# Expert stages: where each engine reads the expert numbers it addresses its operands with

## The chip, the cores and the metric

The kernel runs on one core of a Trainium2 chip. The metric is the device time of one execution in microseconds (us); the time quoted for a kernel is the median of its runs. The engines are named as the profile names them: PE (matrix multiplication; PEld is its weight load), DVE (vector), ACT (activations and copies), POOL (here it issues indirect DMAs) and SP (here it issues DMAs). A name with a q behind it (DVEq, ACTq, SPq) is the part of an engine that reads its instruction stream: it hands work to the engine, and carries out register loads, register arithmetic and branches itself.

## The reference

A block of a network over x of shape 2 x 2048 x 128, in float32. The two `ffn` lines are mixtures of eight experts; each token takes two of them.

```python
x = x + attn_a(layernorm(x))     # windowed attention, 16 heads of 64
x = x + ffn(layernorm(x))        # experts, first time
x = x + attn_b(layernorm(x))     # full attention per batch
x = x + ffn(layernorm(x))        # experts, second time

def ffn(x, w_router, w1, b1, w2, b2):
    probs = softmax(x @ w_router)              # 8 experts
    topk_w, topk_idx = top_k(probs, 2)
    weights = sum(topk_w[..., None] * one_hot(topk_idx, 8), axis=1)
    h = gelu(einsum('te,ieh->tih', x, w1) + b1)   # 128 -> 512
    out = einsum('tih,ihe->tie', h, w2) + b2      # 512 -> 128
    return sum(out * weights[..., None], axis=1)
```

## The kernel before, in words

The stages follow one another: layer norm, windowed attention, an expert stage (`expert_stage`, tag 1), layer norm, full attention, a second expert stage (tag 3). A router inside the attention stages has by then sorted the tokens by expert into a DRAM buffer `xg`, in 40 groups of 256 rows (`GROUPS`), each group of one expert only, and has left two tables in on-chip memory: `emap[j]`, the expert of group j, and `gmap[j]`, the place of group j in `xg`. Which expert a group has is known only at run time, so an engine that addresses weights by it first reads the number from `emap` into a register of its own. `expert` (L1199) does that for DVE and ACT, `place` (L1202) reads `gmap` for SP. One such read is a TENSOR_LOAD, one or two register operations (FUSED_REGOPS) and a range test (SEQ_ASSERT); all of them stand in the trace under L1200 or L1203.

The 40 groups are cut into five turns of eight (`STEP`): turn 0 and turn 4 are written out, turns 1 to 3 are a hardware loop (`rounds`, L1189). `steps` (L1175) builds a turn for PE, ACT and DVE from a `body(jj, k)`. What the engines do for a group:

- SP fetches a group's rows into `xt`, five groups ahead, into one of eight buffers, once POOL's write of the buffer's former group has landed (L1211, L1219).
- PE transposes a group into `px` (L1256), multiplies it with the first weights into `ph` (L1265, 12 products per group) and the result with the second weights into `py` (L1283, 16 products). In body j it does `px` of group j+2, then `ph` of j+1, then `py` of j. There is one `px`, so the `px` of group j+2 waits until DVE has read group j+1's: `pe.wait_ge(S["xl"], START + j + 2)` (L1271).
- ACT copies `px` to `xh` (L1297) for group j+2 and then applies gelu with the expert's bias (L1302) for group j+1.
- DVE copies the expert's first weights to `w1s` (L1324, L1325) and forms `xl` from `px` and `xh` (L1329) for group j+2; then adds the second bias to `py` and scales the result, `yo` (L1337, L1342), for group j-1; then copies the second weights to `w2s` (L1333) for group j+1.
- POOL writes `yo` out with two indirect DMAs per group (L1242).

All this order is written out by hand; each engine runs its own instructions in that order, and semaphores are waited on as counts. Before the change, `turn` in `steps` reads every expert number that the turn needs in one row, before the first group's body: on DVE ten in turn 0, eleven in turns 1 to 3 and nine in turn 4; on ACT nine (eight in turn 4); on SP `turn` reads up to eight places first.

Of the kernel before, what the change touches and what calls it, by code (L numbers as in the profile page):

```python
# [28 lines left out]
STEP = 8  # L29
HCHUNKS = FFN // P  # L30
GROUP = 2 * P
GROUPS = TILES * P * TOPK // GROUP + EXPERTS
# [170 lines left out]
def fetch_outputs(sp, s, got):  # L203

    parts = s.yt.rearrange("(r t p) d -> r p t d", r=TOPK, p=P)
    for i in range(NSB):
        r = slice(i * SB_TILES, (i + 1) * SB_TILES)
        for k in range(TOPK):
            sp.dma_start(got[:, k, r, :], parts[k][:, r, :]).then_inc(s.fetched[i], 16)  # L209


def combine(nc, ch, s, got, i, nth):

    r = slice(i * SB_TILES, (i + 1) * SB_TILES)
    ch.eng.wait_ge(s.fetched[i], 16 * TOPK * nth)
    for k in range(TOPK):
        ch.link(nc.vector.tensor_tensor(s.x[:, r, :], s.x[:, r, :], got[:, k, r, :], ALU.add))  # L217
# [928 lines left out]
def expert_stage(nc, sems, tag, s, result=None):  # L1146
# [5 lines left out]
    with ExitStack() as ctx:  # L1152
        m = Memory(nc, ctx)
        LEAD = 5
# [17 lines left out]
        xg = s.xg[nth]  # L1172
        block = ctx.enter_context(nc.Block())

        def steps(eng, body, ahead=None, behind=False):  # L1175


            def turn(jj):
                es = []
                if ahead is not None:  # L1180
                    es = [expert(eng, STEP * jj + a) for a in range(STEP + ahead)
                          if not isinstance(jj, int) or STEP * jj + a < GROUPS]
                before = [expert(eng, STEP * jj - 1) if not isinstance(jj, int) or jj > 0 else None] if behind else []
                for k in range(STEP):
                    body(jj, k, *([es[k:]] if es else []), *([(before + es)[k]] if behind else []))

            rounds(eng, turn)

        def rounds(eng, turn):  # L1189
            turn(0)  # L1190
            with eng.Fori(0, ROUNDS - 2) as i:
                turn(i + 1)
            turn(ROUNDS - 1)

        def outside(jj, k, ahead):

            return isinstance(jj, int) and not 0 <= STEP * jj + k + ahead < GROUPS

        def expert(eng, j):  # L1199
            return eng.value_load(s.emap[0:1, bass.ds(j, 1)], min_val=0, max_val=EXPERTS - 1)  # L1200

        def place(eng, j):  # L1202
            return eng.value_load(s.gmap[0:1, bass.ds(j, 1)], min_val=0, max_val=XBLOCKS - 1)  # L1203

        def rows(dram, j):
            return dram[bass.ds(j, 1), :, :].rearrange("o (p r) d -> p (o r) d", r=GROUP // P)

        @block.sync
        def _(sp):
            def fetch(g, k):  # L1210
                sp.dma_start(xt[:, k, :, :], rows(xg, g)).then_inc(load[k], 16)  # L1211

            def turn(jj):
                gs = [place(sp, STEP * jj + LEAD + a) if not outside(jj, a, LEAD) else None for a in range(STEP)]
                for k in range(STEP):
                    if not outside(jj, k, LEAD):
                        if not outside(jj, k, LEAD - STEP):
                            was = k + LEAD - STEP
                            sp.wait_ge(put[was % STEP], 32 * (nth * ROUNDS + jj + 1 + was // STEP))  # L1219
                        fetch(gs[k], (k + LEAD) % STEP)  # L1220

            for k in range(LEAD):
                fetch(place(sp, k), k)
            rounds(sp, turn)
            if result is not None:
                for k in range(STEP):
                    sp.wait_ge(put[k], 32 * (nth + 1) * ROUNDS)
                fetch_outputs(sp, s, got)
                for i in range(NSB):
                    sp.wait_ge(summed, START + i + 1)  # L1230
                    r = slice(i * SB_TILES, (i + 1) * SB_TILES)
                    sp.dma_start(tokens[:, r, :], s.x[:, r, :]).then_inc(s.s_out, 16)
                sp.wait_ge(s.s_out, 16 * NSB)
# [59 lines left out]
        @block.scalar  # L1293
        def _(act):
            def read(j, k):
                act.wait_ge(S["t"], START + j + 1)
                nc.scalar.copy(xh[:, k % 2, :], px[:, 0:GROUP]).then_inc(S["xT"], 1)  # L1297

            def gelu(j, k, e):
                act.wait_ge(S["h"], START + j + 1)  # L1300
                for i in range(HCHUNKS):
                    nc.scalar.activation(hT[:, k % 2, i, :], ph[:, k % 2, i, :], ACT.Gelu_apprx_tanh,  # L1302
                                         bias=s.b1[:, bass.ds(e * HCHUNKS + i, 1)]).then_inc(S["gelu"], 1)

            def body(jj, k, es):
                j = STEP * jj + k
                if not outside(jj, k, 2):
                    act.wait_ge(S["h"], START + j + 1)
                    read(j + 2, k + 2)
                if not outside(jj, k, 1):  # L1310
                    if not outside(jj, k, -1):
                        act.wait_ge(S["y"], START + j)
                    gelu(j + 1, k + 1, es[1])

            e = expert(act, 0)
            read(0, 0)
            read(1, 1)
            gelu(0, 0, e)
            steps(act, body, 1)

        @block.vector
        def _(dve):
            def first_weights(j, k, e):
                nc.vector.tensor_copy(w1s[:, k % 2, 0, :], s.w1h[:, e, :])  # L1324
                nc.vector.tensor_copy(w1s[:, k % 2, 1, :], s.w1[:, e, :].bitcast(F32R)).then_inc(S["w1"], 1)  # L1325

            def low_x(j, k):
                dve.wait_ge(S["xT"], START + j + 1)
                nc.vector.tensor_tensor(xl[:, k % 2, :], px[:, 0:GROUP], xh[:, k % 2, :].bitcast(F32),  # L1329
                                        ALU.subtract).then_inc(S["xl"], 1)  # L1330

            def second_weights(j, k, e):
                nc.vector.tensor_copy(w2s[:, k % 2, :, :], s.w2[:, e, :, :]).then_inc(S["w2"], 1)  # L1333

            def keep(j, k, e):
                dve.wait_ge(S["y"], START + j + 1)
                nc.vector.tensor_tensor(yo[:, k % YBUF, :, :], py[:, k % 2, 0:GROUP].rearrange("p (r d) -> p r d", d=P),  # L1337
                                        s.b2[:, bass.ds(e, 1), :].to_broadcast([P, GROUP // P, HID]),
                                        ALU.add).then_inc(S["yb"], 1)
                dve.wait_ge(S["yb"], START + j + 1)  # L1340
                for r in range(GROUP // P):
                    ins = nc.vector.tensor_scalar(yo[:, k % YBUF, r, :], yo[:, k % YBUF, r, :],  # L1342
                                                  xt[:, k % STEP, r, HID + 1:], None, ALU.mult)
                ins.then_inc(S["yo"], 1)

            def body(jj, k, es, e_before):
                j = STEP * jj + k
                if not outside(jj, k, 2):
                    dve.wait_ge(S["h"], START + j + 1)
                    first_weights(j + 2, k + 2, es[2])  # L1350
                    low_x(j + 2, k + 2)
                if not outside(jj, k, -1):
                    if not outside(jj, k, -1 - YBUF):
                        was = k - 1 - YBUF
                        dve.wait_ge(put[was % STEP], 32 * (nth * ROUNDS + jj + 1 + was // STEP))
                    keep(j - 1, (k - 1) % STEP, e_before)
                if not outside(jj, k, 1):
                    if not outside(jj, k, -1):
                        dve.wait_ge(S["y"], START + j)
                    second_weights(j + 1, k + 1, es[1])  # L1360

            e0, e1 = expert(dve, 0), expert(dve, 1)
            first_weights(0, 0, e0)
            first_weights(1, 1, e1)
            low_x(0, 0)
            low_x(1, 1)
            second_weights(0, 0, e0)
            steps(dve, body, 2, behind=True)
            dve.wait_ge(put[(GROUPS - 1 - YBUF) % STEP], 32 * (nth * ROUNDS + (GROUPS - 1 - YBUF) // STEP + 1))
            keep(GROUPS - 1, GROUPS - 1, expert(dve, GROUPS - 1))  # L1370
            if result is not None:
                ch = Chain(dve, s.signals["last"]["chain"])
                for i in range(NSB):
                    combine(nc, ch, s, got, i, 2)
                    dve.sem_inc(summed, 1)
# [459 lines left out]
```

## Time and profile before

| | us |
|---|---|
| median of 3 runs | 1534.84 (1534.63 to 1535.37) |
| the profiled execution, its own time | 1529.88 |
| the profiled execution, its span | 1528.1 |
| busy: PE | 1273.1 (83%) |
| busy: DVE | 1043.8 (68%) |
| busy: ACT | 900.7 (59%) |
| busy: POOL | 763.8 (50%) |

The busy shares are means over stages with different limits. The two expert stages stand in the span from about 811 to 995 us and from about 1327 to 1500 us; what matters for the change is read there. The profile lists TensorE's granted clock as a share of its full 2.4 GHz; half of it is the lower level of 1.2 GHz.

### The profile page before, as it was taken

To read this page: it belongs to the slowest core of one execution; us is meant where nothing else is said; L and a number is where in the kernel's file an instruction comes from. 1 tells how busy PE (TensorE), PEld (TensorE's weight loads), DVE (VectorE), ACT (ScalarE), POOL (GpSimd) and SP (SyncE) were. 2 spreads that over 40 slices of the span, in tenths; PEclk is the share of its full clock that TensorE was granted. 3 is DMA by queue.
4 is the path that set the end of the run, shared out by engine and by line. 5 is a ranking of instruction groups with operands and counts; after the bars stand their busy time and mean duration, and the time that the engine had idled before them with its cause. 6 is when DMAs were issued, how large, how long until landed. Compare 5 with 4: busy or idle time off the path is not lost. (4 is left out here: it accounts for less than half of the span.)

```text
span 1528.1 us, 34022 instructions
## 1 busy us (share of the span) xinstructions
PE 1273.1 (83%) x9640; PEld 1004.4 (66%) x9640; DVE 1043.8 (68%) x3646; ACT 900.7 (59%) x2287; POOL 763.8 (50%) x798
## 2 busy tenths in 40 slices
PE   3999999999999999999956888629878885288892
PEld 2677766777666666766745888616765665288892
DVE  7666877878788787887854554476786788245564
ACT  2677767778686777777753444317655664144451
POOL 3676676686666857667633544400021422434452
PEclk9899999999999999999977999859989997598896
DMA  8999990000000000000031222030000000121226
GB/s 257 209 207 204 202 196 9 4 12 1 10 6 4 12 1 15 1 4 12 2 129 56 64 60 58 25 110 1 1 17 13 29 15 15 46 59 54 60 63 166
DMA packets 129396, 91.94 MB, mean 60 GB/s; under 512 B 9115, under 2 KB 122030, under 8 KB 128992
## 3 DMA queue, kind: packets, MB, share of 16 engines
q1 hardware_dynamic: 118080, 71.84, 21.7%
q0 software_dynamic: 9248, 16.94, 3.3%
q10 hardware_dynamic: 1920, 1.60, 0.3%
q8 instruction: 42, 0.69, 0.2%
q14 instruction: 106, 0.87, 0.2%
HBM read 30.86 MB, written 61.64 MB: 61 GB/s over the span
## 5 line engine op out<-in xcount | busy, mean ns | idle before, releaser
L923 DVE CUSTOM_DVE_ANT_0 sc<-ps,mask 128x256 f32<-128x256 f32 x512 | 196.5, 421 | 155.5 <-PE ps L730 132.8
L842 ACT ACTIVATE sc<-sc,mx 128x256 f32<-128x256 f32 x512 | 255.0, 501 | 37.2 <-DVE mx L923 33.8
L1078 POOL TENSOR_TENSOR rot<-rot,sin 128x512 f32<-128x512 f32 x128 | 177.8, 1389 | 174.0 <-DVE rot L932 173.8
L1242 POOL DMA_INDIRECT yt<-yo,xt x160 | 160.1, 1000 | 201.7 <-DVE yo L1342 172.2
L534 POOL DMA_INDIRECT xg<-r_xw,r_slot x128 | 126.6, 989 | 171.4 <-DVE r_slot L511 131.5
L850 ACT COPY pT<-pt 128x512 f32<-128x512 f32 x256 | 149.6, 584 | 93.1 <-PE pt L740 84.6
L730 PE MATMUL ps<-K,Q 64*128 64x256 f32 x1024 | 190.9, 432 | 13.4 <-DVE mx L923 13.4
L1302 ACT ACTIVATE hT<-ph,b 128x256 f32<-128x256 f32 x320 | 125.4, 476 | 87.2 <-PE ph L1265 87.2
L740 PE MATMUL pt<-ident,sc 128*128 128x128 f32 x1024 | 168.5, 287 | 0.9 <-ACT sc L842 0.6
L753 PE MATMUL po<-pT,V 128*64 128x128 f32 x2048 | 168.8, 286 | 0.0
L1283 PE MATMUL py<-w2s,hT 128*128 128x128 f32 x1280 | 164.8, 284 | 0.6 <-ACT hT L1302 0.6
L740 PEld LDWEIGHTS pt<-ident,sc 128*128 128x128 f32 x1024 | 108.0, 141 | 84.1 <-issue 54.9
L1283 PEld LDWEIGHTS py<-w2s,hT 128*128 128x128 f32 x1280 | 159.2, 202 | 1.4 <-ACT hT L1302 1.4
L753 PEld LDWEIGHTS po<-pT,V 128*64 128x64 f32 x2048 | 106.9, 136 | 65.1 <-issue 33.6
L1265 PE MATMUL ph<-xh,w1s 128*128 128x256 f32 x640 | 145.7, 310 | 0.0
L730 PEld LDWEIGHTS ps<-K,Q 64*128 64x128 f32 x1024 | 86.2, 186 | 58.3 <-issue 36.2
L1265 PEld LDWEIGHTS ph<-xh,w1s 128*128 128x128 f32 x640 | 114.2, 207 | 0.0
L936 DVE TENSOR_TENSOR lin<-lin,cos 128x512 f32<-128x512 f32 x128 | 107.9, 843 | 0.0
L1297 ACT CAST xh<-px 128x256 fp32r<-128x256 f32 x80 | 29.9, 374 | 123.0 <-PE px L1256 80.7
L842 ACT ACTIVATION_READ_ACCUMULATOR sc<-sc,mx 128x1 f32 x512 | 97.5, 190 | 0.0
L1496 PEld LDWEIGHTS bpo<-bV,bpT 128*128 128x128 f32 x544 | 79.7, 210 | 24.9 <-issue 20.8
L1256 PE MATMUL px<-ident,xt 128*128 128x128 f32 x160 | 34.1, 298 | 74.0 <-DMA xt<-xg 38.9
(235 smaller groups left out, 2749.9 us busy)
## 6 DMA issues: line engine op xcount, KB each, us to landing
xg<-zeros SPq DMA_DIRECT2D x76, 520.0 KB, 9.8
xt<-xg SPq DMA_DIRECT2D x80, 130.0 KB, 2.1
got<-yt SPq DMA_DIRECT2D x32, 256.0 KB, 4.6
yt<-yo,xt POOLq DMA_INDIRECT x160, 2.2
xg<-r_xw,r_slot POOLq DMA_INDIRECT x128, 2.3
w<-in_w SPq DMA_DIRECT2D x1, 2048.0 KB, 8.5
out_x<-x SPq DMA_DIRECT2D x8, 256.0 KB, 4.2
x<-in_hidden SPq DMA_DIRECT2D x6, 256.0 KB, 8.4
```

What stands on the lines that cost most here:

```text
L534: self.nc.gpsimd.indirect_dma_start(out=rows, out_offset=bass.IndirectOffsetOnAxis(ap=self.slot[:, self.buf(g), r, t:t + 1], axis=0), in_= ...
L730: ins = nc.tensor.matmul(ps[:, h, 0:2 * P], Q[r, c % QBUF, b * P:(b + 1) * P], K[r, c, b * P:(b + 2) * P], start=True, stop=True)
L740: ins = nc.tensor.transpose(pt[:, b % 2, h, kb, :], sc[:, b, h, kb * P:(kb + 1) * P], s.ident[:, :])
L753: ins = nc.tensor.matmul(po[h * HD:(h + 1) * HD, c % 2, b * P:(b + 1) * P], V[:, c, b + kb, h, :], pT[:, b % 2, h, kb, :], start=(kb == 0) ...
L842: nc.scalar.activation(sc[:, b, h, :], sc[:, b, h, :], ACT.Exp, scale=-1.0, bias=mx[:, b, h:h + 1], accum_out=ls[:, c % 2, b, h:h + 1]).th ...
L850: nc.scalar.copy(pT[:, b % 2, :, :, :], pt[:, b % 2, :, :, :]).then_inc(S["pt"], 1)
L923: nc.vector.tensor_tensor_reduce(sc[:, b, h, :], ps[:, h, 0:2 * P], (mask0 if b == 0 else mask)[:, :], -float(HD) ** -0.5, 3e38, ALU.add, ...
L1078: nc.gpsimd.tensor_tensor(rot[:, which, :], rot[:, which, :], s.sin[:, pos(sb)], ALU.mult).then_inc(S["pool"], 1)
L1242: nc.gpsimd.indirect_dma_start(out=s.yt, out_offset=bass.IndirectOffsetOnAxis(ap=xt[:, k, r, HID:HID + 1].bitcast(U32), axis=0), in_=yo[:, ...
L1265: ins = nc.tensor.matmul(ph[:, k % 2, i, :], w[a], x[:, k % 2, :], start=(n == 0), stop=(n == 2))
L1283: ins = nc.tensor.matmul(py[:, k % 2, r * P:(r + 1) * P], hT[:, k % 2, i, r * P:(r + 1) * P], w2s[:, k % 2, i, :], start=(i == 0), stop=(i ...
L1302: nc.scalar.activation(hT[:, k % 2, i, :], ph[:, k % 2, i, :], ACT.Gelu_apprx_tanh, bias=s.b1[:, bass.ds(e * HCHUNKS + i, 1)]).then_inc(S[ ...
```

## The change

The reads at the head of a turn are removed. In their place `steps` gives the body a function, `expert_of(a)`, that reads the number of the turn's group a when it is first asked for, and keeps it for the rest of the turn. On DVE that puts a read ahead of the first weights of each group (group k+2, before the wait for `h`), and in the first two groups of a turn also reads for the groups that the former turn had known (k-1 and, in the first, k+1). On ACT one read stands between the copy to `xh` and the gelu. On SP each place is read just before the wait and the fetch that use it. The number of reads stays at 110 on DVE and 80 on SP; ACT makes one fewer per turn, since the first of the nine was used by nothing.

```diff
-        def steps(eng, body, ahead=None, behind=False):
+        def steps(eng, body, reads=False):
             def turn(jj):
-                es = []
-                if ahead is not None:
-                    es = [expert(eng, STEP * jj + a) for a in range(STEP + ahead)
-                          if not isinstance(jj, int) or STEP * jj + a < GROUPS]
-                before = [expert(eng, STEP * jj - 1) if not isinstance(jj, int) or jj > 0 else None] if behind else []
+                known = {}
+
+                def expert_of(a):
+
+                    if a not in known:
+                        known[a] = expert(eng, STEP * jj + a)
+                    return known[a]
+
                 for k in range(STEP):
-                    body(jj, k, *([es[k:]] if es else []), *([(before + es)[k]] if behind else []))
+                    body(jj, k, *([expert_of] if reads else []))
...
             def turn(jj):
-                gs = [place(sp, STEP * jj + LEAD + a) if not outside(jj, a, LEAD) else None for a in range(STEP)]
                 for k in range(STEP):
                     if not outside(jj, k, LEAD):
+                        g = place(sp, STEP * jj + LEAD + k)
                         if not outside(jj, k, LEAD - STEP):
                             was = k + LEAD - STEP
                             sp.wait_ge(put[was % STEP], 32 * (nth * ROUNDS + jj + 1 + was // STEP))
-                        fetch(gs[k], (k + LEAD) % STEP)
+                        fetch(g, (k + LEAD) % STEP)
...
-            def body(jj, k, es):
+            def body(jj, k, expert_of):
                 j = STEP * jj + k
                 if not outside(jj, k, 2):
                     act.wait_ge(S["h"], START + j + 1)
                     read(j + 2, k + 2)
                 if not outside(jj, k, 1):
+                    e = expert_of(k + 1)
                     if not outside(jj, k, -1):
                         act.wait_ge(S["y"], START + j)
-                    gelu(j + 1, k + 1, es[1])
+                    gelu(j + 1, k + 1, e)
...
-            def body(jj, k, es, e_before):
+            def body(jj, k, expert_of):
                 j = STEP * jj + k
                 if not outside(jj, k, 2):
+                    e = expert_of(k + 2)
                     dve.wait_ge(S["h"], START + j + 1)
-                    first_weights(j + 2, k + 2, es[2])
+                    first_weights(j + 2, k + 2, e)
                     low_x(j + 2, k + 2)
...
-                    keep(j - 1, (k - 1) % STEP, e_before)
+                    keep(j - 1, (k - 1) % STEP, expert_of(k - 1))
                 if not outside(jj, k, 1):
                     if not outside(jj, k, -1):
                         dve.wait_ge(S["y"], START + j)
-                    second_weights(j + 1, k + 1, es[1])
+                    second_weights(j + 1, k + 1, expert_of(k + 1))
```

Three places show how the instructions move. The line numbers of the changed kernel are 3 to 5 higher; L1203 there is L1200 here. "ISA" rows are register operations and waits.

The first place is DVE at the head of a loop turn. Before, the row of eleven reads ends like this, and the first group's weights and `xl` follow it:

```order
L1200 TENSOR_LOAD emap
L1200 ISA x3
L1200 TENSOR_LOAD emap
L1200 ISA x2
L1324 ISA
L1324 COPY w1s<-w1h 128x512
L1325 REGISTER_ALU
L1325 COPY w1s<-w 128x512
L1329 TENSOR_TENSOR xl<-px,xh 128x256
```

Now one read stands there, and the second follows behind `xl`:

```order
L1203 TENSOR_LOAD emap
L1203 ISA x2
L1328 ISA
L1328 COPY w1s<-w1h 128x512
L1329 REGISTER_ALU
L1329 COPY w1s<-w 128x512
L1332 REGISTER_ALU
L1333 TENSOR_TENSOR xl<-px,xh 128x256
L1360 REGISTER_ALU
L1203 ISA
L1203 TENSOR_LOAD emap
L1203 ISA x2
```

Ten of the eleven reads have left the place ahead of the turn's first `w1s` and `xl`; the first group of a turn now holds three of them and the second holds two.

The second place is DVE in the later groups of a loop turn, from the end of one group (`w2s`) to the next group's `xl`. Before:

```order
L1333 REGISTER_ALU
L1333 COPY w2s<-w 128x512
L1324 ISA
L1324 COPY w1s<-w1h 128x512
L1325 REGISTER_ALU
L1325 COPY w1s<-w 128x512
L1329 TENSOR_TENSOR xl<-px,xh 128x256
```

Now:

```order
L1337 REGISTER_ALU
L1337 COPY w2s<-w 128x512
L1203 ISA
L1203 TENSOR_LOAD emap
L1203 ISA x2
L1328 ISA
L1328 COPY w1s<-w1h 128x512
L1329 REGISTER_ALU
L1329 COPY w1s<-w 128x512
L1332 REGISTER_ALU
L1333 TENSOR_TENSOR xl<-px,xh 128x256
```

A read of one number has come between the copy to `w2s` and the copy to `w1s` of every group.

The third place is ACT in a loop turn, from the copy to `xh` to the first gelu of a group. Before, in every group:

```order
L1297 CAST xh<-px 128x256
L1302 ISA
L1302 ACTIVATE hT<-ph,b 128x256
L1302 ISA
L1302 ACTIVATE hT<-ph,b 128x256
```

Now:

```order
L1300 CAST xh<-px 128x256
L1203 ISA
L1203 TENSOR_LOAD emap
L1203 ISA x2
L1305 ISA
L1305 ACTIVATE hT<-ph,b 128x256
L1305 ISA
L1305 ACTIVATE hT<-ph,b 128x256
```

One read has come between the copy and the gelu of every group, and the nine ahead of the turn's first copy are gone.

## Rows read from the trace of the kernel before

**Rows 1.** The page, its first line.

```profile
span 1528.1 us, 34022 instructions
```

**Rows 2.** Windows over both expert stages: start:end, length, busy us, PEclk, DMA.

```profile
822.00:975.00 153.00, 136.32 (x1113) 135.37 (x1114) 84.49 (x262) 71.56 (x187) 72.13 (x72) 0.93 0.20 58
1338.00:1492.00 154.00, 137.38 (x1112) 136.43 (x1113) 84.81 (x261) 71.54 (x186) 72.23 (x72) 0.92 0.20 58
```

**Rows 3.** Timeline, PE inside turn 0: start us, us, engine, line, operation.

```profile
843.46 0.38 PE L1256 MATMUL px<-ident,xt 128*128 128x128 f32 x2
...
846.89 0.38 PE L1256 MATMUL px<-ident,xt 128*128 128x128 f32 x2
```

**Rows 4.** Timeline, PE's py of groups 0, 8, 9, 10, 37 and 0, 37.

```profile
822.07 2.05 PE L1283 MATMUL py<-w2s,hT 128*128 128x128 f32 x16 [0.18 <-ACT hT L1302]
...
851.97 1.95 PE L1283 MATMUL py<-w2s,hT 128*128 128x128 f32 x16
...
859.98 3.18 PE L1283 MATMUL py<-w2s,hT 128*128 128x128 f32 x16
...
864.65 1.95 PE L1283 MATMUL py<-w2s,hT 128*128 128x128 f32 x16
...
974.72 1.95 PE L1283 MATMUL py<-w2s,hT 128*128 128x128 f32 x16
...
1337.97 2.05 PE L1283 MATMUL py<-w2s,hT 128*128 128x128 f32 x16 [0.39 <-ACT hT L1302]
...
1491.81 1.95 PE L1283 MATMUL py<-w2s,hT 128*128 128x128 f32 x16
```

**Rows 5.** PE's transposes, whole span: idle us before them, times, and until what.

```profile
  DMA xt<-xg: 38.9, 2
  DVE xl L1329: 35.1, 12
```

**Rows 6.** Timeline, DVE and PE from turn 0 to turn 1 [idle before <-releaser].

```profile
848.96 0.42 DVE L1333 COPY w2s<-w 128x512 f32 x1
...
856.77 0.43 DVE L1324 CAST w1s<-w1h 128x512 fp32r x1 [7.39 <-issue]
...
857.45 0.42 DVE L1329 TENSOR_TENSOR xl<-px,xh 128x256 fp32r<-128x256 f32 x1
...
857.92 0.44 PE L1256 MATMUL px<-ident,xt 128*128 128x128 f32 x2 [4.00 <-DVE xl L1329]
```

**Rows 7.** L1200, 848 to 858 us: count, ns min/median/max, first and last start.

```profile
L1200 DVEq TENSOR_LOAD <-emap x11: 300/304/319, 848.9 to 856.0; - x11
L1200 ACTq TENSOR_LOAD <-emap x9: 272/282/380, 849.4 to 854.5; - x9
```

**Rows 8.** L1200 at the end of a stage: one read by itself, and DVE beside it.

```profile
L1200 DVEq TENSOR_LOAD <-emap x1: 302/302/302, 980.6 to 980.6; - x1
L1200 DVEq FUSED_REGOPS  x1: 190/190/190, 980.9 to 980.9; - x1
...
980.56 0.49 DVE L1342 TENSOR_SCALAR yo<-yo,xt 128x128 f32<-128x128 f32 x2
```

**Rows 9.** Timeline, DVE and ACT inside turn 0.

```profile
845.46 1.57 ACT L1302 ACTIVATE hT<-ph,b 128x256 f32<-128x256 f32 x4 [1.15 <-PE ph L1265]
...
847.77 0.43 DVE L1329 TENSOR_TENSOR xl<-px,xh 128x256 fp32r<-128x256 f32 x1 [1.16 <-ACT xh L1297]
```

**Rows 10.** SP's waits, 826 to 990 us (us, times, longest); POOL's timeline.

```profile
SPq L1211 <- DMA yt<-yo,xt: 106.1, 29, 9.9
...
846.47 1.00 POOL L1242 DMA_INDIRECT yt<-yo,xt  x1 [1.15 <-DVE yo L1342]
```

**Rows 11.** The loop's jump back: DVE's last copy, and its next read.

```profile
882.18 0.42 DVE L1333 COPY w2s<-w 128x512 f32 x1
...
L1200 DVEq TENSOR_LOAD <-emap x1: 314/314/314, 882.4 to 882.4; - x1
```

**Rows 12.** Window behind the stall of turn 1: PEclk is third from the end.

```profile
859.00:863.00 4.00, 4.00 (x23) 4.00 (x22) 2.87 (x10) 1.57 (x4) 2.83 (x3) 0.57 0.12 37
```

More of the change, by code:

```diff
@@ L1318, in _ @@
             gelu(0, 0, e)
-            steps(act, body, 1)
+            steps(act, body, reads=True)
         @block.vector
@@ L1367, in _ @@
             second_weights(0, 0, e0)
-            steps(dve, body, 2, behind=True)
+            steps(dve, body, reads=True)
             dve.wait_ge(put[(GROUPS - 1 - YBUF) % STEP], 32 * (nth * ROUNDS + (GROUPS - 1 - YBUF) // STEP + 1))
```

## The prediction

> **What bounds the kernel now.** The span is 1528.1 us [rows 1], and the change touches only the two expert stages, so I read those. Inside a turn PE is the bound: its transposes for two neighbouring groups start 3.43 us apart (843.46 and 846.89), and the one runs into the next without a gap [rows 3]. If all groups went at that pitch, 37 of them would take 126.9 us. The list of PE's `py` products shows what they take: from group 0 to group 37 the first stage needs 974.72 - 822.07 = 152.75 us and the second 1491.81 - 1337.97 = 153.84 us [rows 4]. The difference, 25.7 + 26.9 = 52.7 us, is what both stages lose against their own steady pitch. The windows over the same stretches agree: PE is busy for 136 of 153 us, at a granted clock of 0.92 to 0.93 [rows 2].
>
> Where it is lost can be seen at a change of turn. `py` of group 9 comes 8.01 us after that of group 8, and that of group 10 another 4.67 us later, where 3.43 would do: 4.6 + 1.2 us [rows 4]. The timeline of the place tells why. DVE ends a group with its `w2s` copy at 848.96 and starts nothing until 856.77; the profile names no other engine for that gap of 7.39 us ("issue"), and PE's transpose waits 4.00 us for the `xl` behind it [rows 6]. In those 7.8 us stand eleven register reads of DVE, from 848.9 on, 0.71 us apart (7.1 us over ten steps), of which the TENSOR_LOAD itself is 0.30 us [rows 7]. ACT makes nine, 0.64 us apart (5.1 us over eight steps), at the same time [rows 7]. Over both stages PE's transposes waited 35.1 us for `xl` in 12 places [rows 5]: one small wait in each stage is that of its very first groups, the other ten are the head of turn 0 and the four changes of turn. The rest of the 52.7 us is the clock: after that stall the window shows a mean granted clock of 0.57, that is nearly all of it at the lower level of 1.2 GHz [rows 12], and `py` of group 9 takes 3.18 us instead of 1.95 [rows 4].
>
> **The change part by part.** *Removed at the heads:* with one read left ahead of `w1s`, the ten stalls of PE and the stretches at 1.2 GHz behind them go, if what is put back is hidden. Worth 52.7 us at most.
>
> *DVE, added per group: one read.* By the row at the head it costs 0.71 us [rows 7]. That it costs more alone than in a row has a row too: at the end of the stage DVE makes one read by itself, 0.302 us, and does so while its engine is busy with `yo` (980.56, the read at 980.6) [rows 8]; so the read neither waits for the engine nor holds it up. Of each 3.43 us DVE idles 1.16 us, before `xl`, until ACT's `xh` is there [rows 9]. The read stands ahead of that idle time, behind `w2s`, so it comes out of it: 0.71 of 1.16 us if nothing of it overlaps, less if it runs under `w2s`, as it did at 848.9. Bounds: 0 and 0.71 us per group on DVE, both 0 on PE. What covers it is that idle time; without it each of some 74 groups would be 0.71 us longer, 53 us, the whole gain.
>
> *DVE, first two groups of a turn:* three reads and two, 5 x 0.71 = 3.55 us against 2 x 1.16 = 2.32 us, so DVE may fall 1.2 us behind, once per turn. Queued behind these reads are `yo` and `w2s`, and then the next group's `xl`, for which PE's transpose waits. That has a cushion: `xl` ends at 847.77 + 0.43 = 848.20 [rows 9], and the transpose that needs it comes one pitch after 846.89 [rows 3], at 850.32, so 2.1 us later. From the third group on DVE gains 0.45 us per group and has caught up by the fifth. I take 0 on PE; if the cushion were gone it would be 1.2 us for each of eight changes of turn, 9.8 us.
>
> *ACT, added per group: one read,* 0.64 us [rows 7], between `xh` and gelu, where ACT idles 1.15 us for PE's `ph` [rows 9]. It costs 0; without the cover 0.64 us per group. One read fewer per turn is off any path.
>
> *SP, one place ahead of each wait.* SP spends 106.1 us in 29 waits for POOL's writes, 3.7 us each [rows 10], and a read spends part of that wait. PE waited for a fetched group twice in the whole span, at the first group of each stage [rows 5]. POOL, whose writes free the buffers, idles 1.15 us per group at the steady pitch [rows 10], so this ring needs no pause at the turns. 0.
>
> *Turn 0* loses its head of ten reads in the same way, and is inside the 52.7 us. PE and POOL have the same instructions as before.
>
> *Sum:* 52.7 us less 0. The profiled execution's own 1529.88 would become 1477.2. Its runs' median is 4.96 us above it; I carry that over: 1534.84 - 52.7 = **1482.1 us**.
>
> One page speaks against the size of the added reads. The Trainium skill, "Runtime: NRT & Kernel Launch", section on the preamble and postamble breakdown, gives TENSOR_LOAD about 1.3 us, for register loads from HBM. This case's rows show 0.30 us for reads of a table in on-chip memory, and the measurement decides. By the page's figure a read would be 1.3 + 0.41 us, as an estimate, which is 0.55 us over DVE's idle time, and 74 groups would give back 41 us of the gain.
>
> **The rivals.** *(a) The heads still stall.* The five reads of a turn's first two groups end on PE after all. For it speaks that DVE has more to do there than its idle time holds; against it the 2.1 us cushion. Eight times 1.2 us: 1492 us.
>
> *(b) The loop's jump back shows.* Before, it lay under PE's work and the reads. At 882.18 DVE starts its last copy of a loop turn, and its next read stands at 882.4 [rows 11]: 0.2 us, no stall, which speaks against it. For it: the loop bodies of DVE, ACT and SP have grown and moved. The nearest row for an upper price is PE's stall of 4.00 us at a change of turn [rows 6]; with two jumps back per stage, four in all, that is up to 16 us: 1498 us. The same page of the Trainium skill, section on instruction fetch, says that a taken branch to a page of code that is no longer held waits for a fetch; the jump in this trace shows none.
>
> *(c) No change.* The pause at a turn is when the ring of fetches and writes catches up, and would come back as a wait for `xt`. SP's longest wait of 9.9 us [rows 10] speaks for a ring that is not far ahead, POOL's idle time and PE's two waits [rows 5] against it. About 1535 us.
>
> *(d) Slower.* A read between DVE's instructions costs far more than in a row, since DVE's stream must start again after it. The cover is 1.16 us per group, and 52.7 us over 74 groups is another 0.71; above 1.87 us per read the kernel would be slower than before. At 2.5 us it would be 74 x 1.34 = 99 - 53 = 46 us slower, 1581 us. Against it stands the single read of 0.302 us [rows 8]; the rows do not show when the next instruction went to the engine behind it.
>
> **How the numbers follow.** The forecast, all reads hidden, has 0.78; (a) 0.09; (b) 0.05; (c) 0.03; (d) 0.05. A change of less than 0.2% (3 us) is about what a measurement of this kernel cannot tell from none. Forecast, (a) and (b) are faster by more than that: 0.92 faster, 0.03 same, 0.05 slower. The range reaches up to (b), 1497 us, and takes in the 9.8 us of the heads; down to 1478, where the runs would lie if the 4.96 us between profile and median went with the stalls. With (c) and (d) outside, and some doubt about the lower end, it leaves out somewhat over one in ten. The forecast's own range is 1479 to 1486.
>
> **What the profile of the changed kernel would show.** `py` of groups 0 to 37 should take 127 to 129 us in each stage, at a granted clock near 1.00, and PE's transposes should wait for `xl` next to nothing but once at each stage's start. DVE's idle time before `xl` should fall from 1.16 to between 0.4 and 1.1 us, with "issue" gone as what ends it. Each read should still be 0.30 us. If PE waits for `xl` in the second or third group of a turn, (a) holds; only in turns 2 and 3, (b); for `xt`, (c); a pitch above 3.43 us in every group is (d). What would make the prediction wrong above all: that the 2.1 us cushion of `xl` is not there when three reads fall together.

## The result, and the profile after

The changed kernel takes 1485.93 us (median of 4 runs, 1481.23 to 1489.22) against 1535.11 us before (median of 4, 1534.63 to 1540.97). The ratio is 0.9675 with a 95% interval of 0.965 to 0.970, so 46 to 54 us of 1535.11 are gone. Forecast were 1482.1 us and 52.7 us less.

The windows over both expert stages of the changed kernel, from `py` of group 0 to that of group 37 (start:end, length, busy us of PE, PEld, DVE, ACT and POOL, PEclk, DMA); they answer to [rows 2]:

```profile
824.00:951.00 127.00, 126.63 (x1106) 126.63 (x1107) 88.02 (x257) 72.26 (x187) 75.10 (x72) 1.00 0.23 67
1316.00:1443.00 127.00, 127.00 (x1110) 127.00 (x1111) 88.66 (x258) 71.83 (x186) 74.57 (x72) 1.00 0.24 68
```

PE is busy throughout, and the granted clock is 1.00 where it was 0.92 to 0.93. The `py` products at both ends of the two stages, from the timeline of the changed kernel, as in [rows 4]:

```profile
824.37 2.05 PE L1286 MATMUL py<-w2s,hT 128*128 128x128 f32 x16 [0.49 <-ACT hT L1305]
...
951.50 1.95 PE L1286 MATMUL py<-w2s,hT 128*128 128x128 f32 x16
...
1315.94 2.05 PE L1286 MATMUL py<-w2s,hT 128*128 128x128 f32 x16 [0.50 <-ACT hT L1305]
...
1443.08 1.95 PE L1286 MATMUL py<-w2s,hT 128*128 128x128 f32 x16
```

951.50 - 824.37 = 127.13 us and 1443.08 - 1315.94 = 127.14 us, where it was 152.65 and 153.84: 25.5 + 26.7 = 52.2 us less, and 37 groups at 3.43 us are 126.9. What ended PE's idle time before its transposes, over the whole span of the changed kernel, as in [rows 5]:

```profile
  DMA xt<-xg: 39.5, 2
  DVE xl L1333: 1.8, 2
```

Of the twelve waits for `xl` with 35.1 us, two with 1.8 us are left, those of the first groups of each stage. The wait for a fetched group is as before.

The span of this execution is 1479.5 us, 48.6 less than before, not 52.2. The other 3.6 us lie outside the stretches above: the first `py` starts 2.3 us later (824.37 against 822.07 [rows 4]), the second stage's follows 364.44 us after group 37 of the first instead of 363.25, and the rest is the end. Whether the change has this price or executions merely scatter by it is what the first two runs below ask.

Where the reads lie now is seen on DVE. First a group inside turn 0 of the changed kernel: its read (L1203 in a window over the group: count, ns min/median/max, first and last start) and DVE's timeline beside it.

```profile
L1203 DVEq TENSOR_LOAD <-emap x1: 309/309/309, 841.8 to 841.8; - x1
...
841.66 0.48 DVE L1346 TENSOR_SCALAR yo<-yo,xt 128x128 f32<-128x128 f32 x2
842.06 0.42 DVE L1337 COPY w2s<-w 128x512 f32 x1
842.52 0.43 DVE L1328 CAST w1s<-w1h 128x512 fp32r x1
...
844.30 0.42 DVE L1333 TENSOR_TENSOR xl<-px,xh 128x256 fp32r<-128x256 f32 x1 [1.02 <-ACT xh L1300]
```

The read starts at 841.8, while DVE still works on `yo` and has not begun `w2s`; only some 0.1 us of it shows between `w2s` and `w1s`, whose starts are 0.46 us apart here and 0.34 in the kernel before (842.09 and 842.43). The idle time before `xl` is 1.02 us, down from 1.16 [rows 9]. Then the change of turn (turn 0 to turn 1) of the changed kernel, DVE and PE, to be laid beside [rows 6]:

```profile
848.92 0.42 DVE L1337 COPY w2s<-w 128x512 f32 x1
849.63 0.43 DVE L1328 CAST w1s<-w1h 128x512 fp32r x1 [0.28 <-issue]
...
851.12 0.42 DVE L1333 TENSOR_TENSOR xl<-px,xh 128x256 fp32r<-128x256 f32 x1 [0.72 <-ACT xh L1300]
852.27 0.42 DVE L1341 TENSOR_TENSOR yo<-py,b 128x256 f32<-128x256 f32 x1 [0.73 <-issue]
...
853.56 0.43 DVE L1337 COPY w2s<-w 128x512 f32 x1 [0.34 <-issue]
853.72 0.38 PE L1259 MATMUL px<-ident,xt 128*128 128x128 f32 x2
...
854.41 0.43 DVE L1328 CAST w1s<-w1h 128x512 fp32r x1 [0.42 <-issue]
...
855.22 0.41 DVE L1333 TENSOR_TENSOR xl<-px,xh 128x256 fp32r<-128x256 f32 x1
...
857.16 0.38 PE L1259 MATMUL px<-ident,xt 128*128 128x128 f32 x2
```

The three reads of the turn's first group show as "issue": 0.28 us before `w1s`, 0.73 before `yo`, 0.34 before `w2s`. The 0.42 us before the next `w1s` are the second group's first read. The second `xl` comes at 855.22, 0.67 us later than one pitch after 851.12, and is done at 855.63; PE needs it at 857.16 and does not wait.

### The profile page after: what moved, and what is told of

Its sections match the earlier page's. It is cut to its first block and busy times, and to the rows that moved or that the text cites. A ratio compares the mean times of both kernels' runs of the same rounds, so it can differ in the third digit from the quotient of the medians.

```text
span 1479.5 us, 34018 instructions
## 1 busy us (share of the span) xinstructions
PE 1257.6 (85%) x9640; PEld 989.7 (67%) x9640; DVE 1055.1 (71%) x3646; ACT 901.5 (61%) x2287; POOL 770.8 (52%) x798
## 5 line engine op out<-in xcount | busy, mean ns | idle before, releaser
L1245 POOL DMA_INDIRECT yt<-yo,xt x160 | 166.6, 1041 | 143.0 <-DVE yo L1346 112.9
L1286 PE MATMUL py<-w2s,hT 128*128 128x128 f32 x1280 | 156.3, 275 | 1.0 <-ACT hT L1305 1.0
L1286 PEld LDWEIGHTS py<-w2s,hT 128*128 128x128 f32 x1280 | 150.0, 192 | 1.8 <-ACT hT L1305 1.8
L1268 PE MATMUL ph<-xh,w1s 128*128 128x256 f32 x640 | 137.7, 298 | 0.0
L1268 PEld LDWEIGHTS ph<-xh,w1s 128*128 128x128 f32 x640 | 107.6, 195 | 0.0
L932 DVE STREAM_SHUFFLE rot<-lin 128x512 f32<-128x512 f32 x128 | 94.1, 735 | 0.2
L1268 PE MATMUL ph<-xl,w1s 128*128 128x256 f32 x320 | 91.8, 287 | 0.0
```

Of the source, the lines that this page charges most:

```text
L1245: nc.gpsimd.indirect_dma_start(out=s.yt, out_offset=bass.IndirectOffsetOnAxis(ap=xt[:, k, r, HID:HID + 1].bitcast(U32), axis=0), in_=yo[:, ...
L1268: ins = nc.tensor.matmul(ph[:, k % 2, i, :], w[a], x[:, k % 2, :], start=(n == 0), stop=(n == 2))
L1286: ins = nc.tensor.matmul(py[:, k % 2, r * P:(r + 1) * P], hT[:, k % 2, i, r * P:(r + 1) * P], w2s[:, k % 2, i, :], start=(i == 0), stop=(i ...
```

## The experiments

**Twice the same kernels.** Both kernels were run again unchanged, with profiles. Before:

> The kernel before, unchanged, for a second profile. Both expert stages of the changed kernel ran at PE's pitch and gave back 52.2 us, but its span is only 48.6 us shorter: the stretch ahead of the first stage's first py was 2.3 us longer and the one between the stages 1.2 us longer. If those 3.6 us are scatter between executions, this profile shows the first py of the first stage anywhere from 821 to 826 us (822.07 in the first profile) and the stages still 152 to 154 us each; if they are a price of the change, this profile repeats 822.07 and 363.3 us from py 37 of the first stage to py 0 of the second to within 0.5 us. Time 1535 us.

After:

> The changed kernel, unchanged, for a second profile and a better interval. Both theories of the 3.6 us expect 127.1 us from py 0 to py 37 in each stage. Scatter: the first py between 821 and 826 us. Price of the change: again 824.4 us, and 364.4 us between the stages. Time 1486 us, ratio 0.965 to 0.970.

In the second execution of the kernel before, `py` of the first group stands here in the timeline:

```profile
830.18 2.05 PE L1283 MATMUL py<-w2s,hT 128*128 128x128 f32 x16 [0.79 <-ACT hT L1302]
```

That is 8.1 us later than in the first execution of the same kernel, more than the range that I had set for scatter. From there to group 37 it took 154.75 us, and 153.60 in the second stage; 363.47 us lie between the stages. The changed kernel's second execution has its first `py` at 826.95, twice 127.14 us in the stages, and 362.31 us between them. So each stage repeats to some 2 us before and to 0.01 us after, while the first `py` moves by 8.1 us before and 2.6 after, and the stretch between the stages by 0.2 and 2.1. The 3.6 us can't be told from that scatter; a price of the change is not shown. Times: the kernel before 1.0017 of itself (0.9991 to 1.0043), the changed kernel 1483.75 us, ratio 0.9632 (0.9598 to 0.9666).

**Only DVE reads late.** `steps` gets the reads that are to be made ahead of the first body of a turn:

```diff
-        def steps(eng, body, reads=False):
+        def steps(eng, body, reads=False, first=()):
...
+                for n in first:
+                    if not outside(jj, 0, n):
+                        expert_of(n)
                 for k in range(STEP):
                     body(jj, k, *([expert_of] if reads else []))
...
+                gs = [place(sp, STEP * jj + LEAD + a) if not outside(jj, a, LEAD) else None for a in range(STEP)]
...
-                        g = place(sp, STEP * jj + LEAD + k)
+                        g = gs[k]
...
-            steps(act, body, reads=True)
+            steps(act, body, reads=True, first=range(STEP + 1))
```

> The changed kernel, with ACT's nine reads and SP's eight back at the head of each turn; only DVE reads late. Theory (DVE's and ACT's heads run side by side, and the later one sets the stall): ACT's xh at a change of turn is still about 4.7 us late, 2.3 us less than DVE's xl was, so PE stalls about 2 us at each of eight changes of turn instead of 4.0 to 4.4, with less time at the low clock behind it, and keeps the loss at turn 0's head: 20 to 28 us of the 52 stay, 1506 to 1514 us. Rival (DVE's head is the whole cause): as the changed kernel, 1486 us.

Measured: 1519.88 us, ratio 0.9862 (0.9822 to 0.9902). The rival is out, and the theory's price was too low: each stage takes 142.6 and 143.1 us, 31 us over the changed kernel's together, where 20 to 28 were expected. The timeline at the change from turn 1 to turn 2 shows a part that was left out:

```profile
898.00 0.37 ACT L1304 CAST xh<-px 128x256 fp32r<-128x256 f32 x1 [4.75 <-issue]
898.40 0.43 DVE L1337 TENSOR_TENSOR xl<-px,xh 128x256 fp32r<-128x256 f32 x1 [4.92 <-ACT xh L1304]
898.88 0.44 PE L1263 MATMUL px<-ident,xt 128*128 128x128 f32 x2 [2.17 <-DVE xl L1337]
...
900.71 0.43 DVE L1341 COPY w2s<-w 128x512 f32 x1 [0.34 <-issue]
...
901.24 2.02 PE L1290 MATMUL py<-w2s,hT 128*128 128x128 f32 x16 [0.49 <-issue]
```

PE's stall for `xl` is 2.17 us, as expected. But `xl` is now so late that DVE's own two reads, behind `xl` and before `w2s`, are no longer covered: `w2s` ends at 901.14, and `py`, idle for another 0.49 us, starts 0.10 us later. The clock did not fall behind this stall; a window there (PEclk is third from the end):

```profile
900.00:905.00 5.00, 4.50 (x40) 4.33 (x39) 4.06 (x13) 2.04 (x6) 2.48 (x3) 1.00 0.08 26
```

At the change from turn 0 to turn 1 of the same execution it did, behind a stall that was no longer:

```profile
867.49 0.44 PE L1263 MATMUL px<-ident,xt 128*128 128x128 f32 x2 [2.12 <-DVE xl L1337]
...
869.00:871.00 2.00, 2.00 (x11) 2.00 (x11) 1.24 (x4) 0.32 (x1) 0.98 (x1) 0.50 0.00 0
```

By the pitch of `py`, the changes into turn 1, where the clock fell in both stages, cost 3.9 and 4.1 us, the four into turns 2 and 3, where `py` waits as above at a full clock, some 3.2 each, the two into turn 4 some 1.4 each, and the heads of turn 0 cost 4.0 and 4.3 us.

**Only ACT reads late.** The same edit, with DVE's eleven numbers at the head:

```diff
-            steps(dve, body, reads=True)
+            steps(dve, body, reads=True, first=(*range(STEP + 2), -1))
```

> The changed kernel, with DVE's reads and SP's back at the head of each turn; only ACT reads late. Theory (the later of the two heads sets the stall, and DVE's is the later): the stalls at the changes of turn stay at 4.0 to 4.4 us, only turn 0 gains a little: 1530 to 1536 us. Rival (each engine's head costs its own share): half of the gain, near 1510 us.

Measured: 1536.37 us, ratio 0.9976 (0.9945 to 1.0006): 0.4 us above the theory's upper end, far from the rival, and a time that can't be told from the kernel before. PE's waits over the span of this kernel:

```profile
  DVE xl L1337: 31.3, 12
```

31.3 of 35.1 us are still there. The stages take 152.20 and 150.23 us; what they gained against the kernel before lies in turn 0, where `py` of group 1 follows 0.65 us late instead of 2.4 to 3.1. PE's wait for `xl` at the head of turn 0, first stage, with only DVE late and then with only ACT late:

```profile
836.11 0.44 PE L1263 MATMUL px<-ident,xt 128*128 128x128 f32 x2 [2.10 <-DVE xl L1337]
```

```profile
835.56 0.44 PE L1263 MATMUL px<-ident,xt 128*128 128x128 f32 x2 [0.31 <-DVE xl L1337]
```

In both profiles of the kernel before, this wait is 2.10 us too. So at the head of turn 0 ACT's row sets the stall, and at the four changes of turn DVE's does, with ACT's under it. The two heads don't add up: taking out ACT's alone is worth some 4 us (the stages of the kernel before repeat to 2), DVE's alone 21 us (52.2 less 31), both together 52.

**SP's reads back at the head.** Of the edit of the run with only DVE late, just the lines with `gs`; DVE and ACT read late:

> The changed kernel, with SP's eight reads of places back at the head of each turn; DVE and ACT read late. Theory (SP's reads lie in its waits for POOL's writes): no wait of PE for a fetched group beyond the first of each stage, 127 us per stage, 1486 us. Rival (with the pauses gone the fetches are short of time): PE waits for xt at the changes of turn, up to 8 x 4 us, 1490 to 1518 us.

Measured: 1481.62 us, ratio 0.9633 (0.9582 to 0.9684), 127.14 us in each stage. SP's waits between 826 and 970 us (us, times, longest), first of the changed kernel, then of this one:

```profile
SPq L1214 <- DMA yt<-yo,xt: 80.0, 32, 10.0
```

```profile
SPq L1217 <- DMA yt<-yo,xt: 79.5, 29, 7.7
```

The wait for POOL's writes is as long either way: SP's part of the change is worth nothing that could be measured.

**Two and three reads per group.** The number ahead of each `first_weights` is read once more, or (with `range(2)`) twice more, into a register that nothing uses:

```diff
                     e = expert_of(k + 2)
+                    for _ in range(1):
+                        expert(dve, j + 2)
```

> The changed kernel; DVE reads the number ahead of each first_weights twice. Theory A (a read runs under yo's and w2s' work on the engine, so DVE has some 1.6 us per group for reads before PE's pitch gives way, and 1.42 us fits): pitch 3.43 us in every group, at most some small stalls at the heads, 1486 to 1491 us. Theory B (as predicted: each read comes wholly out of the 1.16 us of idle time, and 1.42 us is 0.26 too much): pitch about 3.7 us, 74 x 0.26 = 19 us, 1505 us.

> The changed kernel; DVE reads the number ahead of each first_weights three times. Theory A (some 1.6 us per group are free): in the loop turns 2.13 us of reads are about 0.5 us too much, in turns 0 and 4, where a read is some 0.6 us, 0.1 us: pitch 3.9 and 3.5 us, 48 x 0.5 + 26 x 0.1 = 27 us, 1513 us. Theory B (1.16 us are free): 0.97 us too much per group, 72 us, 1558 us.

Two reads: 1483.63 us, ratio 0.9649 (0.9613 to 0.9685), 127.14 us in each stage. Three: 1513.03 us, ratio 0.984 (0.9803 to 0.9877), stages of 140.25 and 139.75 us, 25.7 us more. Theory A holds in both sums (1483.63 us lies 2.4 below its range, as the other runs at 127.14 us do), theory B, which is the way the prediction counted, in neither. Two reads are free but not without a trace: in the loop turns `xl` is then ready as little as 0.6 us before PE needs it, where one read leaves 1.5. What ended PE's idle time before its transposes, with two reads and then with three:

```profile
  DVE xl L1333: 1.8, 2
```

```profile
  DVE xl L1333: 11.3, 20
```

How the 25.7 us are spread was not as A had it: most groups of the loop turns come some 0.2 to 0.3 us late, not 0.5, and the two groups behind each change into a loop turn lose some 2 us together, where the turn's first two groups hold five and four reads.

**Seven reads at the head, four in the middle.**

```diff
+                    if ahead:
+                        for n in ahead.get(k, ()):
+                            if not outside(jj, 0, n):
+                                expert_of(n)
                     body(jj, k, *([expert_of] if reads else []))
...
-            steps(dve, body, reads=True)
+            steps(dve, body, reads=True, ahead={0: (2, -1, 1, 3, 0, 4, 5), 4: (6, 7, 8, 9)})
```

> The changed kernel; DVE reads seven numbers ahead of the first group of a turn and four ahead of the fifth, ACT and SP read late. Theory A (1.6 us free per group, and xl may come 2.1 us late before PE waits): the four are hidden, the seven (5.0 us in a loop turn) are 1.3 us too much: six stalls of 1.3 us and two of 0.5, with the clock kept, 9 us, 1495 us; up to 1502 us if the clock falls behind each. Rival (no cushion: all beyond the idle time stalls PE): 3.8 and 1.7 us per turn, some 40 us, 1526 us.

Measured: 1495.32 us, ratio 0.9715 (0.9671 to 0.9758); stages of 132.86 and 132.77 us, 11.4 us more than the changed kernel's, where 9 were expected. Theory A holds. Its timeline at two changes of turn, and a window behind the first:

```profile
858.17 0.43 DVE L1332 CAST w1s<-w1h 128x512 fp32r x1 [4.61 <-issue]
...
859.33 0.44 PE L1263 MATMUL px<-ident,xt 128*128 128x128 f32 x2 [1.22 <-DVE xl L1337]
...
888.44 0.44 PE L1263 MATMUL px<-ident,xt 128*128 128x128 f32 x2 [1.43 <-DVE xl L1337]
...
859.00:864.00 5.00, 4.67 (x41) 4.68 (x42) 4.61 (x16) 2.31 (x6) 2.42 (x3) 1.00 0.12 35
```

In the loop turns 1.2 to 1.5 us of the seven reads reach PE, of the four none: only the head of each turn has late `py` products, by 1.4 to 1.8 us in the loop turns and 0.8 to 0.9 in turn 4. The clock stays at its full level.

## Why the prediction was right

*The loss at the heads.* 52.7 us were read from the pitch of `py`, 52.2 came back: every change of turn now passes at 3.43 us. That this was a chain of reads, ending in `xl` and PE, and not the fetches, is shown by putting rows back: with DVE's (only ACT late) nearly all of the loss is back, with ACT's (only DVE late) 31 us of it, and with SP's alone nothing. The prediction named ACT's nine reads and gave them no part in the loss. They set the stall at the head of turn 0, and without DVE's row they would have kept 31 of the 52 us; since the change took out both, the sum did not suffer.

*One read per group.* Its cost on PE was put at 0 and is 0. The argument for it was too tight: its bound took the read to come out of the 1.16 us for which DVE idles. Inside turn 0 all but some 0.1 us of it runs under the engine's work on `yo` and `w2s`, since DVE's instruction stream is ahead of its engine there. The Trainium skill, "Perfetto Trace Analysis", section on the DVE / Act engine instruction, says that once an instruction is pushed to the wait queue the sequencer is ready for the next; the read at 841.8 agrees. Where the prediction would have had two reads cost 19 us, they cost nothing, and three cost 26 instead of 72.

*The first two groups of a turn.* DVE was to fall 1.2 us behind against a cushion of 2.1; it falls 0.67 us behind, and `xl` is ready 1.5 us before PE needs it. Rival (a) had only the cushion against it. The cushion is real but not wide: seven reads in a row, or an `xl` that is 2 us late for another reason (only DVE late), go through it.

*The clock.* Its share came back with the stalls, as forecast. In the kernel before, the 4.00 us stall was followed by a mean granted clock of 0.57 [rows 6, 12]; stalls of up to 1.54 us with seven reads at the head were followed by 1.00. In between, the length of the stall doesn't decide: with only DVE late, stalls of 2.12 and 2.35 us before turn 1 were followed by stretches at 0.50, the lower level, and four of 2.17 to 2.22 us before turns 2 and 3 by 1.00. What else decides is open.

*The other rivals.* (b): the pitch is 3.43 us across both jumps back of each loop, so they don't show on PE. (c): PE waits for a fetch twice, as before. (d): the pitch is 3.43 us in every group, so a single read has no cost on PE at all. Its TENSOR_LOAD takes hardly longer than in a row; the median of all 110 of DVE in the changed kernel is 0.309 us against 0.304 [rows 7], in this row of L1203 over the whole span:

```profile
L1203 DVEq TENSOR_LOAD <-emap x110: 297/309/568, 813.3 to 1448.9; - x110
```

The 1.3 us that the Trainium skill, "Runtime: NRT & Kernel Launch", section on the preamble and postamble breakdown, gives for register loads from HBM thus don't hold for this table in on-chip memory.

*The sum.* 1482.1 us against 1485.93, 1483.75 and, with SP's reads at the head, 1481.62. The difference is within what either kernel scatters by outside the expert stages, where nothing was changed. The changed kernel's median lies 4.7 us above its profiled execution (1485.93 and 1481.23), so the 4.96 us that were carried over fit. Two slips stand in the prediction and move nothing: 974.72 - 822.07 is 152.65, not 152.75 (the 25.7 us follow from 152.65), and the upper end of its range, 1497 us, is called (b), which it had priced at 1498. One sign was wrong: "issue" has not gone from DVE's waits; at the change of turn it has been cut into pieces of 0.3 to 0.7 us.

## What to carry to other kernels

When an engine reads run-time numbers into registers, a row of reads can stop that engine for as long as the row (eleven reads left DVE idle for 7.39 us here), while single reads beside the work that needs them can cost nothing, as long as the engine's stream has time between its instructions. Look for "issue" as the cause of an idle time and count the register reads in it. When two engines have such rows at the same place, fix both: the shorter one is hidden under the longer, and appears when that is gone. What a stall of PE costs is more than its length if the clock falls behind it, which here it did behind some stalls of 2 us and not behind others; compare the pitch of one repeated product across the place with the pitch elsewhere.

## What the runs showed that I had not expected

A second read per group is free on DVE although the engine has 1.16 us of idle time and two reads take 1.42: the stream reads ahead of the engine. And the start of the first expert stage moved from 822.07 to 830.18 us between two executions of one kernel, while the stages themselves, once PE set their pace, repeated to 0.01 us in four of four stretches in the two profiles of the changed kernel.
